# A decoder layer with routed experts: first stage batch by batch, a new opening, a shorter routing chain, and seventeen unread products

## The reference

```python
x = x + attn(layernorm(x))               # 16 heads of 16; softmax over the 4 rows of axis 0
x = x + xattn(layernorm(x), ctx, ctx)    # 16 heads of 64; 64 context rows for each of 4
x = x + ffn(layernorm(x))                # 8 experts, each takes its 256 rows of 2048

# attn: q = x Wq; logits = -|q_t - q_s|^2 / sqrt(16) for each head; weights = softmax over s
#       PXAV = weights (x A) Wv, with A = Wq Wq^T / sqrt(16) for each head; result = PXAV out_w^T + out_b
# ffn:  route_prob = softmax(xf Ws + bs).T            # (8, 2048)
#       vals, routes = top_k(route_prob, 256)         # each expert chooses its rows
#       out = gelu(xf[routes] W1 + b1) W2 + b2
#       final = zeros.at[routes].add(out * vals)
```

## Time and profile before

| | us |
|---|---|
| median of 3 runs | 398.11 (396.01 to 398.89) |
| the profiled execution | 402.48 |
| its span, first to last instruction | 400.7 |
| TensorE busy | 324.4 (81%) |
| VectorE busy | 291.9 (73%) |
| GpSimd busy | 188.4 (47%) |
| ScalarE busy | 186.2 (46%) |
| mean granted clock | 0.908 |

### The profile page before, as it was taken

How to read it: one execution, slowest core, us unless ns; L and a number is a source line. 1 busy time by engine, 2 the same in 40 slices (tenths; PEclk the granted TensorE clock), 3 DMA queues, 4 the chain that set the end, 5 groups by cost and what they waited for, 6 DMA issues and landing times.

```text
span 400.7 us, 6340 instructions
## 1 busy us (share of the span) xinstructions
PE 324.4 (81%) x2280; PEld 289.2 (72%) x2280; DVE 291.9 (73%) x659; ACT 186.2 (46%) x359; POOL 188.4 (47%) x244
## 2 busy tenths in 40 slices
PE   1988787796798999999999974111599999999991
PEld 0766675564465999999999974001599999999991
DVE  1576688646578898888888862887647889799860
ACT  2546754142356446657566462236032575462330
POOL 3565677601202363887887873500503344434333
PEclk9999999597999999999999997555579999999997
DMA  8930000000000013521512534400115686723222
GB/s 244 404 118 2 1 0 2 0 0 0 2 2 0 2 33 113 171 74 72 185 42 92 185 119 127 163 0 1 52 39 201 166 253 141 242 40 55 28 26 26
DMA packets 24046, 34.27 MB, mean 86 GB/s; under 512 B 1784, under 2 KB 20560, under 8 KB 23888
## 3 DMA queue, kind: packets, MB, share of 16 engines
q1 hardware_dynamic: 20112, 29.36, 21.7%
q0 software_dynamic: 3072, 4.20, 6.1%
q10 hardware_dynamic: 832, 0.32, 0.4%
HBM read 27.58 MB, written 6.29 MB: 85 GB/s over the span
## 4 chain that ended last, share of the span: by engine, by line
PE 71%; DVE 15%; ACT 6%; issue 3%; DMA 2%; POOL 1%; SPq 0%; DVEq 0%; POOLq 0%; ACTq 0%
PE bank L888 12%; PE bank L890 11%; PE bank L889 11%; PE bank L724 5%; PE q_banks L706 4%; PE q_banks L888 4%; PE q_banks L890 4%; PE q_banks L889 4%; PE bank L909 3%; DVE flags_all L1228 2%; PE bank L1385 2%; PE bank L740 2%; DMA wva<-in_L_attn_v_weight 2%; PE bank L953 1%; PE bank L855 1%
## 5 line engine op out<-in xcount | busy, mean ns | idle before, releaser
L1500 POOL DMA_INDIRECT out_x<-ybuf,idx x16 | 26.6, 1664 | 62.6 <-DVE ybuf L1519 60.4
L1013 POOL TENSOR_TENSOR prob<-prob,rsum 128x1024 f32<-128x1024 f32 x16 | 30.5, 1905 | 18.7 <-DVE rsum L1105 17.2
L888 PE MATMUL bank<-H_hi,PT_hi 128*128 128x256 f32 x128 | 36.3, 284 | 1.7 <-DVE PT_lo L1082 1.7
L888 PE MATMUL bank<-W_hi,h_hi 128*128 128x256 f32 x128 | 37.2, 291 | 0.0
L890 PE MATMUL bank<-H_hi,PT_lo 128*128 128x256 f32 x128 | 36.2, 283 | 0.0
L889 PE MATMUL bank<-H_lo,PT_hi 128*128 128x256 f32 x128 | 36.2, 283 | 0.0
L890 PE MATMUL bank<-W_hi,h_lo 128*128 128x256 f32 x128 | 36.2, 283 | 0.0
L889 PE MATMUL bank<-W_lo,h_hi 128*128 128x256 f32 x128 | 36.2, 283 | 0.0
L1458 ACT ACTIVATE hbuf<-bank,b_cols 128x256 f32<-128x256 f32 x32 | 13.4, 471 | 43.0 <-PE bank L890 43.0
L1481 POOL DMA_INDIRECT xg<-xn_rows,idx x16 | 18.4, 1152 | 31.4 <-DVE idx L1542 26.3
L997 ACT ACTIVATE prob<-prob 128x1024 f32<-128x1024 f32 x16 | 16.9, 1058 | 33.4 <-DVE prob L1126 33.4
(11 more groups left out here) (275 smaller groups left out, 1067.8 us busy)
## 6 DMA issues: line engine op xcount, KB each, us to landing
W_raw<-in_L_ffn_W SPq DMA_DIRECT2D x16, 1024.0 KB, 5.9
X<-in_x SPq DMA_DIRECT2D x4, 512.0 KB, 8.9
xn_rows<-xn SPq DMA_DIRECT2D x16, 128.0 KB, 1.7
out_x<-X SPq DMA_DIRECT2D x4, 512.0 KB, 3.8
Wq<-in_L_xattn_Wq SPq DMA_DIRECT2D x1, 1024.0 KB, 11.7
Wk<-in_L_xattn_Wk SPq DMA_DIRECT2D x1, 1024.0 KB, 13.8
Wv<-in_L_xattn_Wv SPq DMA_DIRECT2D x1, 1024.0 KB, 13.1
Wo<-in_L_xattn_Wo SPq DMA_DIRECT2D x1, 1024.0 KB, 14.4
```

The source lines that it names most:

```text
L888: t.matmul(out_ps, hi, rhs_hi, start=first, stop=False)
L1013: g.tensor_tensor(prob[:, s], prob[:, s], rsum[:, s].unsqueeze(2).to_broadcast([P, HX, CK]), ALU.mult).then_inc(prob_ready, 1)
L1500: g.indirect_dma_start(out_flat, bass.IndirectOffsetOnAxis(ap=idx[:, e, h:h + 1], axis=0), ybuf[:, h], None, bounds_check=ROWS - 1, oob_is ...
```

## The change

*Opening.* SyncE loads batch 1 of `x` ahead of the context and two attention weights. TensorE begins with 34 products of the identity with itself, which nobody reads. VectorE normalises three of the four tiles of batch 0, as soon as the power is done (semaphore `powers`).

*First stage.* Instead of a loop over steps, every engine has its order written out, batch by batch. `dif[1]` gets a place of its own, so batch 1's differences no longer wait for the query weight in whose place they lay; the context and two attention weights lie there first. G products alternate between two pairs of banks, the H products start in others. Batch 3's pair sums and its addition of `q` go to GpSimd, whose second-norm deviations all come behind that. The exponentials of batch `j` wait for `scaled` of the batch before.

*Third norm, last tile*: VectorE normalises it (ScalarE before).

*Routing.* `bits` lies in PSUM. One scan over two rows of ranks in place of two scans; TensorE adds the offset; the values are split by the position itself, for experts 0 and 1 one at a time.

*Experts.* The one-hot of expert 0 comes in two halves. Twelve unread products follow list 1, five follow list 2. The gathers of the two halves of an expert have a semaphore each. For expert 0 the transposed rows lie in two banks and are evacuated in two parts.

```diff
+        wva, owa, ctx_sb = (dif1[:, 2 * i:2 * i + 2] for i in range(3))
+
+        dif = [dif0[:], dif1[:]]
...
             load_x(0)
             sp.dma_start(wqa[:], wq_s).then_inc(ld["wqa"], 16)
-            sp.dma_start(ctx_sb[:], ctx_rows).then_inc(ld["ctx"], 16)
-            sp.dma_start(owa[:], ow_s).then_inc(ld["attw"], 16)
-            sp.dma_start(wva[:], wv_s).then_inc(ld["attw"], 16)
             load_x(1)
+            sp.dma_start(ctx_sb, ctx_rows).then_inc(ld["ctx"], 16)
+            sp.dma_start(owa, ow_s).then_inc(ld["attw"], 16)
+            sp.dma_start(wva, wv_s).then_inc(ld["attw"], 16)
...
                 if j >= 1:
                     act.wait_ge(weighted, j)
+
+                    act.wait_ge(scaled, j)
...
+            normalise(1, (0, 1))
+            q_evac(0, 1)
+            normalise(1, (2, 3))
             ps = bank_full(act, "owT")
             a.activation(owT[:], v3(ps[:], MC), ACT.Copy).then_inc(owT_ready, 1)
-            xnT_evac(0)
-            normalise(1)
-            q_evac(0)
             ps = bank_full(act, "cols")
             a.activation(bias_cols[:], ps[:, 0:3 * NC], ACT.Copy).then_inc(cols_ready, 1)
             a.activation(b1_cols[:], ps[:, 32:32 + E * FC], ACT.Copy).then_inc(cols_ready, 1)
-            ps = bank_full(act, "N")
-            a.activation(Nw[:], v3(ps[:], MC), ACT.Copy).then_inc(Nw_ready, 1)
             squares(0)
...
+            ps = bank_full(act, "N")
+            a.activation(Nw[:], v3(ps[:], MC), ACT.Copy).then_inc(Nw_ready, 1)
+            KV_evac(0)
+            squares(1)
+            xnT_evac(2)
+            weights_of(1)
+            G_evac(0)
+            KV_evac(1)
+            q_evac(2)
+            mixT_evac(0)
+            normalise(3)
+            squares(2)
+            G_evac(1)
+            xnT_evac(3)
+            weights_of(2)
+            KV_evac(2)
+            q_evac(3)
+            mixT_evac(1)
+            G_evac(2)
+            squares(3)
+            weights_of(3)
+            KV_evac(3)
+            G_evac(3)
+            mixT_evac(2)
+            KV_evac(4)
+            G_evac(4)
+            KV_evac(5)
+            G_evac(5)
+            KV_evac(6)
+            mixT_evac(3)
+            G_evac(6)
+            KV_evac(7)
+            G_evac(7)
...
+            for t in range(1, T):
+                i = t * NJ
+                v.tensor_scalar(xn1[:, t], X[:, i], mv[:, i, 0:1], rstd[:, i:i + 1], ALU.subtract,
+                                ALU.mult).then_inc(xn1_ready, 1)
+            for j in (1, 2):
                 dve.wait_ge(ld_x[j], 16)
                 statistics(j, var1_ready)
...
             v.tensor_copy(WqT[:, :, D - 1], bias_cols[:, 0:NC]).then_inc(bq_placed, 1)
             WqT_evac(0)
-            distances(0)
+            weigh(0)
+            differences(1)
...
+            WqT_evac(2)
+            distances(1)
+            WqT_evac(3)
+            scale(0)
+            weigh(1)
+            differences(2)
+            low_parts(0)
+            add_residual(0)
+            distances(2)
+            scale(1)
+            low_parts(1)
+            weigh(2)
+            differences(3)
+            statistics2(0)
+            distances(3)
+            scale(2)
+            low_parts(2)
+            weigh(3)
+            add_residual(1)
+            low_parts(3)
+            statistics2(1)
+            add_residual(2)
+            scale(3)
             low_parts(4)
-            dve.wait_ge(weighted, NJ)
...
+            statistics2(2)
             low_parts(5)
-            add_residual(s - 1)
-            statistics2(s - 1)
             low_parts(6)
-            add_residual(s)
-            statistics2(s)
+            add_residual(3)
             low_parts(7)
...
+
+            for _ in range(WARM_UP):
+                t.matmul(banks[7][:, 0:P], ident[:], ident[:], start=True, stop=True)
+            xn_transpose(0)
...
             KV_product(0)
+            xn_transpose(2)
+            WqT_transpose(3)
+            q_product(2)
...
-                    G_product(c)
+            G_product(0)
+            KV_product(1)
+            mix_transpose(0)
+            pe.wait_ge(Nw_ready, 1)
+            y_product(0)
+            G_product(1)
+            xn_transpose(3)
+            KV_product(2)
+            q_product(3)
+            mix_transpose(1)
+            G_product(2)
+            y_product(1)
+            KV_product(3)
+            G_product(3)
+            mix_transpose(2)
+            KV_product(4)
+            y_product(2)
+            G_product(4)
+            KV_product(5)
+            G_product(5)
+            KV_product(6)
+            mix_transpose(3)
+            G_product(6)
+            y_product(3)
+            KV_product(7)
...
+                if n == NT - 1:
+                    g.tensor_tensor(rstd3[:, s:s + 1], rstd3[:, s:s + 1], neg_half[:, 0:1],
+                                    ALU.pow).then_inc(rstd3_ready, 1)
+                else:
+                    g.tensor_tensor(nmean3[:, s:s + 1], mv3[:, s, 0:1], neg_one[:], ALU.mult)
...
                     v.bn_aggr(mv3[:, s], stats3[:, s]).then_inc(var3_ready, 1)
+                    if n == NT - 1:
+                        dve.wait_ge(var3_ready, NT)
+                        dve.wait_ge(rstd3_ready, NT)
+                        dve.wait_ge(xn3_stored, 16 * NT)
+                        v.tensor_scalar(xn3[:, s], X[:, n, :], mv3[:, s, 0:1], rstd3[:, s:s + 1], ALU.subtract,
+                                        ALU.mult).then_inc(last_xn3_ready, 1)
...
-            v.memset(ones_f[:], 1.0)
+
+            order(v.memset(ones_f[:], 1.0))
+            v.memset(ones_f[:, 1, 0:1], 0.0)
             dve.wait_ge(keysT_full, 1)
             dve.wait_ge(ones_ready, 1)
+
...
-            order(v.tensor_copy(offs[:, 0:3], banks[1][:, 8:11]))
-            order(v.tensor_tensor(offs[:, 1:2], offs[:, 1:2], offs[:, 2:3], ALU.add))
-            v.scalar_tensor_tensor(out=rank_gt[:], in0=rank_gt[:], scalar=offs[:, 0:1], in1=gt[:], op0=ALU.add, op1=ALU.mult)
-            order(v.scalar_tensor_tensor(out=rank_eq[:], in0=rank_eq[:], scalar=offs[:, 1:2], in1=eq[:],
-                                         op0=ALU.add, op1=ALU.mult))
-
-            v.tensor_tensor(keys[:], rank_gt[:], rank_eq[:], ALU.add).then_inc(pos_ready, 1)
+            order(v.tensor_copy(offs[:, 0:2], banks[1][:, 8:10]))
+            for k in range(2):
+                ins = v.scalar_tensor_tensor(out=ranks[:, k], in0=ranks[:, k], scalar=offs[:, k:k + 1], in1=taken[:, k],
+                                             op0=ALU.add, op1=ALU.mult)
+            order(ins)
+            v.tensor_tensor(keys[:], ranks[:, 0], ranks[:, 1], ALU.add).then_inc(pos_ready, 1)
...
+        def split_vals_by_position(e):
+
+            posT = v3(banks[0][:, 0:P], E)[:, e].unsqueeze(2).to_broadcast([P, NT, NV])
+            for h, op in enumerate((ALU.is_lt, ALU.is_ge)):
+                nc.vector.scalar_tensor_tensor(out=vals_h[:, e, :, h], in0=posT, scalar=P + 0.5, in1=vals[:, e],
+                                               op0=op, op1=ALU.mult)
...
+
+            list_of(FIRST_LISTS[0])
+            list_of(FIRST_LISTS[1])
+            idle_products(12)
+            list_of(FIRST_LISTS[2])
+            idle_products(5)
             transposes(EXPERTS[0])
```

More of the change, by code:

```diff
@@ L439, in act_part1, with normalise @@
             a = nc.scalar
-            def normalise(j):
+            def normalise(j, tiles=range(T)):
                 act.wait_ge(rstd1_ready, j + 1)
@@ L443, in normalise @@
                     act.wait_ge(full[1], where[f"T{j - 1}1"][1] + 1)
-                for t in range(T):
+                for t in tiles:
                     i = t * NJ + j
@@ L791, in pe_part1 @@
             WqT_transpose(0)
+            q_product(1)
             WqT_transpose(1)
@@ L985, in act_step @@
                 W_high(act, nth)
-            if old.within(NT):
+            if old.within(NT - 1):
                 s, n = old.slot, old.n
```

273 lines of the change are left out of this document (111 added, 162 removed).

## The result

| | before | change |
|---|---|---|
| median, 20 runs each | 399.2 (395.76 to 402.18) | 395.19 (393.58 to 396.77) |
| profiled execution | 402.48 | 393.97 |
| its span | 400.7 | 392.2 |

The ratio is 0.9914, interval 0.989 to 0.9939: faster by 0.9%, or 2.4 to 4.4 us, where 12.6 were forecast, and outside the forecast's range. The ratios leave out the executions that are over 1.5% above the fastest of their kernel, the medians do not. The two profiled executions differ by 8.5 us, the medians by 4.0.

The account below looks back on a forecast made before the run. The prediction took TensorE to bound the second and fourth stages, waits between four engines the first, and a chain of short steps the routing. Terms -9.5 - 0.6 - 2.5 = -12.6 took 398.11 to 385.5 us, range 380 to 391.

Parts of the forecast that it names:

- the size of stage 1: First stage: end 12.5 us earlier, less 3.0 us for one clock fall, -9.5 us (ends -12.5 and -6.5).
- This end has no loss of clock: First stage's end: second stage's first products start at 94.0 instead of 106.49 us, -12.5 us, no clock fall counted.
- the 4 us that I gave to the opening: First stage's opening: VectorE begins its first differences at 17.9 us, 4 us earlier.
- I take that it falls once: First stage: the 3.2 us wait ahead of batch 2's mix transposes lowers TensorE's clock once, costing 3.0 us.
- Rival A: First stage: the clock holds through the 3.2 us wait; -15.6 us, 382.5 us; chance 0.22.
- the layout: First stage: four engines' new order laid out with traced durations; last G product ends 90.0, second stage starts 94.0 us.
- B: First stage: only the opening comes through, batches stay at 14.25 us; -7.1 us, 391 us; chance 0.14.
- C: Routing to experts: clock stays low through 17 unread products, delaying lists; +2.1 replaces -2.5, 390.1 us; chance 0.10.
- D: First stage: clock falls before batch 2's mix and stays low to the stage's end; 402.8 us; chance 0.03.
- One sign of being wrong: Second or fourth stage: a change of more than 1 us would show the forecast wrong.
- The routing's -2.5: Routing to experts: shorter chain and 17 unread products let expert 0 start at full clock; -2.5 us (ends -2.0 and -3.3).
- xn3's -0.6: Last row of the third norm: ScalarE's 0.60 us becomes one VectorE operation; -0.6 us (ends 0 and -1).

Follow-up runs that it names:

- the second half alone: Kernel before with only the change's last third-norm tile, routing, split one-hot, 17 unread products and xgT in parts, first stage as before: 395.21 us, ratio 0.9894.
- the fills: Unread TensorE products put into first-stage waits: five waits of the change, 387.56 us, ratio 0.9735; three waits of the kernel before, 393.12 us, ratio 0.986.

## Why the prediction was wrong

**The step that failed is the size of stage 1.** The sentence "This end has no loss of clock", behind -12.5, took 94.0 for the end of the new order, rightly, but subtracted it from 106.49, which has 9.4 us in it that belong to that execution: about 7 of clock and about 2 of a load that came late (97.10 with the clock held and the load early, 100.40 in another execution of the same program). The profile had shown the clock's part: the opening at half speed and two y products of 6.59 and 6.11 us. I described these rows and then credited their disappearance to the change, as if the kernel before had them in every execution. The load I overlooked: the row just ahead of those in the earlier trace rows waits 2.97 us for `wva`, and I read the late start of batch 0 as the opening's order. Measured with the clock held on both sides the term is -3.4, or about -5 with a late load, and not -12.5. Nearly all of it lies in the batches; of the 4 us that I gave to the opening 0.2 are left against an early load.

**"I take that it falls once"** failed too. Rival A and the forecast looked at one wait, the 3.2 us ahead of M2 (measured 3.07). The waits that I had laid out ahead of q1 and q2, 2.4 and 1.9 us, came as 2.15 and 1.97 and each lowered the clock: 1.7 us twice. The fall at M2 cost 1.5 and not 3.0, since the clock was back before y2 (3.62 us). A wait of 3.80 ahead of H, which the layout (94.0 less 90.0) contains as well, cost 1.5. Four falls in place of one: H starts at 99.52 instead of 94.0 + 3.0 = 97.0. With the 1.5 us behind it, that is 4.0 of the 4.1 us by which the profiled executions' difference (8.5) misses the forecast's 12.6. I had let two rows decide, 2.78 us that held and 3.43 that fell; q2's 1.97 refutes that, and y0's 2.05 us did not lower the clock in the same trace.

**From one execution to the median.** I carried -12.6 over unchanged. The profiled execution stood 4.4 us above the median that I was given, and I said so, but did not ask what made it so. That was the clock, the very thing that I counted as won, and the late load: 8.5 between the profiled executions is 4.0 between the medians.

What was right: the layout (T0 at 11.88 for 11.6, q1 23.37 for 23.0, differences at 18.17 for 17.9, y0 and later only late by the falls before them); that the batches are shorter, so B's old 14.25 us cycle is out (batch 2 to 3 takes 12.7), and B has it the wrong way round, since against an early load the opening is what brings nothing; `high` at 0.29 us and with it -1.25 for the conversion. Expert 0's products were 0.12 apart, which refutes C. D did not come: after each fall in this trace the clock was back within 5 us. One sign of being wrong was badly chosen: the fourth window changed by 2.7 us, over the 1 us that I had allowed, by the very 2.8 us of expert 0's half clock that I had forecast.

The Trainium skill ("SBUF — State Buffer", Who interferes with whom) says that VectorE in a two-port mode and GpSimd keep each other from the ports that they share, and that an instruction with at most one input in SBUF, outside those modes, stays clear; it does not speak of PSUM there. The trace agrees with both readings of `high`: from SBUF it took 1.22 to 1.94 us in the four profiles that have it so, from PSUM 0.29 in all ten, though GpSimd makes the same table beside it (2.48 us at 244.29 in the change). The three new operations of VectorE in the opening met GpSimd and lost little: 0.42 to 0.56 us each, against 0.41 for an equal one at 239.8.

The routing's -2.5 and xn3's -0.6, 3.1 together, came as 3.3 by the second half alone, with an interval of 2.0 to 6.5. The steps fit too. Counted from the first row of the routing, list 1 starts 1.6 us earlier (32.5 us behind it for 34.0), where 1.65 were forecast. That leaves 0.85 of the 2.5 to the 17 products, and these measured -0.5 in one comparison (faster without them) and 0.8 in the other. How much each small step of the chain gives was not tried.

**The falls, read back.** 395.19 less 387.56, 7.6 us, is what the fills give in the change; 398.49 less 393.12, 5.4, what they give in the kernel before (3.4 to 7.8 by the interval of the ratio). The change makes the order better by 393.12 less 387.56, 5.6 us with the second half's share in it, and by these medians loses 2.2 of this to its own additional waits. The two filled kernels ran on two chips, and the interval is wider than the 2.2, so that its size is not shown. It is median against median, and it is the account that replaces the forecast's.

## What to carry to other kernels

Before a gain is taken from one profiled execution, take the clock and the loads out of both sides: mark every piece of work at half clock and every wait for a load in the profile before, price the kernel without them, and compare with the new order's clean end; then count as a possible fall every wait in the new order that is as long as those that had one in a trace of the kernel (here 1.97 us and up), not the longest alone. An engine that waits for a flag should be followed to what raises the flag: two memsets of 0.06 us, placed behind unrelated work, held up the whole second stage by 3.8 us. A wait is better removed than filled (-2.4 us by the medians at M2), and filled only where it can't be removed.

## What the runs showed of the hardware

The same wait does and does not lower TensorE's clock. Two programs that are alike up to there, both with 2.05 us ahead of y0 and 0.3 us apart in time:

```profile
43.11 3.69 PE L737 MATMUL bank<-Nw,mixT 128*128 128x256 f32 x16 [2.05 <-ACT mixT L491]
```

```profile
42.83 5.38 PE L737 MATMUL bank<-Nw,mixT 128*128 128x256 f32 x16 [2.05 <-ACT mixT L491]
```

The first is the version with masks early and fills, the second the one without the 17 products, which come much later. The change's first stage shows it too: q1 fell behind 2.15 us in the change and held in the version without the 34 products, and q2 fell behind 1.97 in the change and held behind 1.96 in the version without the 17. So part of a kernel's spread is this: the change ran between 393.58 and 396.77 us, the same with its waits filled between 387.49 and 388.88. It is not the whole: the kernel before with its waits filled still ran between 391.93 and 395.99. The Trainium skill ("TensorE: Matmul & The Clock Gate", Part 1) says that the chip's look at TensorE's activity runs free of the kernel's start, so that the point of a change moves between executions; these two rows agree with it. The clock fell in the change behind waits of 1.97 and 2.15 us that have short transposes before them (0.60 us at 34.67, and for q1 0.66 us at 20.56). Whether the transposes have a part in it was not tried.

A load lands at different times in executions of one program. The attention weight was waited for until 7.8 and 8.0 us in two profiled executions of the old opening, and until 10.2 and 10.6 in the other two. What decides it was not looked into.

In the opening the granted clock can read 1.00 while products run at half speed: from 15 to 21 us of the profile before the column has 1.00 in each microsecond in which TensorE was busy, and the q product there took 5.72 us where an equal one took 3.72.
